# A transformer block with linear attention and top-2 experts: the router in natural layout, LayerNorm 2 through a PSUM bank, small steps moved between engines

## The reference, cut to what matters

```python
mod = (silu(c) @ wmod).reshape(2, 6, 1, -1)
sa, ca, ga, sb, cb, gb = mod[:, 0], ..., mod[:, 5]
ga, gb = (2 * (g >= 0) - 1) * maximum(abs(g), 0.25)        # for g in ga, gb
h = layernorm(x) * (1 + ca) + sa
Q, K, V = h @ Wq.T + bq, h @ Wk.T + bk, h @ Wv.T + bv      # 16 heads of 16
Q, K = elu(Q) + 1, elu(K) + 1
Z = 1 / (Q . sum_s(K) + 1e-6)                              # per token and head
x = x + ga * ((Q @ (K^T V) * Z) @ Wo.T + bo)
h = layernorm(x) * (1 + cb) + sb
logits = (h / |h|) @ (centroids / |centroids|).T + h @ w_route.T     # 8 experts
gates = softmax(logits where logits >= second largest, else -inf)
out_e = gelu(h @ w1[e] + b1[e]) @ w2[e] + b2[e]            # exact gelu
x = x + gb * sum_e gates[e] * out_e
```

## Time and profile before

| | us |
|---|---|
| three runs | 414.61, 415.77 (median), 416.47 |
| profiled execution | 416.12 |
| its span, first to last instruction | 414.3 |

### The profile page before, as it was taken

How to read it: one execution, slowest core, us unless ns; L and a number is a source line. 1 busy time by engine, 2 the same in 40 slices (tenths; PEclk the granted TensorE clock), 3 DMA queues, 4 the chain that set the end, 5 groups by cost and what they waited for, 6 DMA issues and landing times. The chain is left out here.

```text
span 414.3 us, 8993 instructions
## 1 busy us (share of the span) xinstructions
PE 359.5 (87%) x2610; PEld 329.2 (79%) x2610; DVE 340.4 (82%) x993; ACT 206.9 (50%) x451; POOL 254.0 (61%) x292
## 2 busy tenths in 40 slices
PE   4998899999996456889899899899898998998695
PEld 3477788888875446889889789789798898998695
DVE  4988778888779988898898898898998988986643
ACT  2256587787662144454554453454545544545341
POOL 2415778878766555766767758658667677465101
PEclk9999899999999977999999999999999999999999
DMA  8944000000000031132321421313223214223301
GB/s 264 331 147 127 2 0 0 0 0 2 1 2 0 1 102 53 52 108 54 97 79 52 127 73 54 117 61 76 93 66 96 77 52 126 78 56 124 105 26 52
DMA packets 23179, 30.36 MB, mean 73 GB/s; under 512 B 2258, under 2 KB 13938, under 8 KB 23156
## 3 DMA queue, kind: packets, MB, share of 16 engines
q1 hardware_dynamic: 22340, 29.03, 23.3%
q10 hardware_dynamic: 816, 1.05, 0.7%
HBM read 25.75 MB, written 4.33 MB: 73 GB/s over the span
## 5 line engine op out<-in xcount | busy, mean ns | idle before, releaser
L448 POOL TENSOR_TENSOR hid_pair<-hid_g,hid_pair 128x512 fp32r<-128x512 f32 x56 | 75.6, 1350 | 67.0 <-ACT hid_pair L619 67.0
L612 ACT ACTIVATE bank<-bank,cols_sb 128x256 f32<-128x256 f32 x128 | 51.3, 438 | 50.7 <-PE bank L662 50.5
L660 PE MATMUL bank<-tr_hi,w_hi 128*128 128x256 f32 x256 | 74.2, 290 | 0.0
L662 PE MATMUL bank<-tr_hi,w_lo 128*128 128x256 f32 x256 | 72.4, 283 | 0.0
L661 PE MATMUL bank<-tr_lo,w_hi 128*128 128x256 f32 x256 | 72.4, 283 | 0.0
L662 PE MATMUL bank<-w_hi,hid_pair 128*128 128x256 f32 x252 | 70.8, 281 | 0.0
L660 PE MATMUL bank<-w_hi,hid_pair 128*128 128x256 f32 x252 | 70.8, 281 | 0.0
L661 PE MATMUL bank<-w_lo,hid_pair 128*128 128x256 f32 x252 | 70.7, 280 | 0.0
L619 ACT ACTIVATE hid_pair<-hid_g 128x512 fp32r<-128x512 f32 x64 | 40.5, 632 | 31.4 <-DVE hid_g L1243 30.3
L1243 DVE TENSOR_TENSOR hid_g<-bank,g_bc 128x512 f32<-128x512 f32 x64 | 43.9, 686 | 10.3 <-ACT bank L612 8.7
L660 PEld LDWEIGHTS bank<-tr_hi,w_hi 128*128 128x128 f32 x256 | 49.1, 192 | 0.6
(11 more groups left out here) (153 smaller groups left out, 927.6 us busy)
## 6 DMA issues: line engine op xcount, KB each, us to landing
g_bc<-g_dram SPq DMA_DIRECT2D x64, 256.0 KB, 3.4
x_sb<-in_x SPq DMA_DIRECT2D x16, 256.0 KB, 3.0
out<-x_sb SPq DMA_DIRECT2D x15, 256.0 KB, 2.3
early<-in_wmod ACTq DMA_DIRECT2D x2, 512.0 KB, 8.0
q_sb<-in_w SPq DMA_DIRECT2D x2, 512.0 KB, 6.4
q_sb<-in_w SPq DMA_DIRECT2D x1, 1024.0 KB, 9.4
q_sb<-in_wqkvT SPq DMA_DIRECT2D x1, 768.0 KB, 6.7
early<-in_wmod SPq DMA_DIRECT2D x1, 512.0 KB, 3.9
```

Of the source, the lines that this page charges most:

```text
L448: gp.tensor_tensor(hid_lo[:, p, :, :], hid_g[:, p % 2, :, :], hid_hi[:, p, :, :].bitcast(F32), ALU.subtract).then_inc(e_hlo, 1)
L612: last = ac.activation(half, half, ACT.Gelu, bias=b1_sb[:, e:e + 1])
L660: te.matmul(out_ap, l_hi, r_hi, start=start, stop=False)
L662: return te.matmul(out_ap, l_lo, r_hi, start=False, stop=stop)
```

## The change

VectorE's share: `stats_of` ends with bn_aggr; `modulate_e` is two operations over both tiles, one in place in PSUM; `gates_a` has no transposes; `gates_b` writes one product; `denominators` loses the eps step and stands after gates_a; `scale_experts` is one operation. ScalarE gains `normalise_e` (x * rstd - mean * rstd into bank 7) and a second gate copy. POOL gains the negated mean, eps and neg_mr for LayerNorm 2, and `lo_gates`, and its order in the step changes. PE's router has the tokens stationary, and both tiles' expert sums share bank 6 (the last unit's second tile uses bank 7). b2's rows are its high, high and low parts at partitions 0, 32 and 64, to match the gates' high, low and high parts.

```diff
-        lgT = bank[1][0:4 * NE, 0:2 * P]
+        xn = bank[7][:, :].rearrange("p (t e) -> p t e", t=2)
+        lg = bank[1][:, 0:8 * NE].rearrange("p (t k) -> p t k", t=2)
+        def sums(u, t):
+            return bank[7][:, 0:E] if t == 1 and u.nth(NU - 1) else bank[6][:, t * E:(t + 1) * E]
+        def kv_bank(u):
+            return bank[2] if u.nth(NU - 1) else bank[6 + u.h]
@@ gpsimd
+            def make_rstd(u, eps, power, done):
+                h = u.h
+                gp.tensor_scalar(neg_mean[:, h, :], mv[:, h, :, 0], -1.0, None, ALU.mult)
+                gp.tensor_scalar(var_eps[:, h, :], mv[:, h, :, 1], LN_EPS, None, ALU.add).then_inc(eps, 1)
+                wait(pool, eps, u.count(1, 1))
+                gp.tensor_tensor(rstd[:, h, :], var_eps[:, h, :], minus_half[:, 0:2], ALU.pow).then_inc(power, 1)
+                wait(pool, power, u.count(1, 1))
+                gp.tensor_tensor(neg_mr[:, h, :], neg_mean[:, h, :], rstd[:, h, :], ALU.mult).then_inc(done, 1)
+            def lo_gates(u):
+                if not u.plus(-1) or u.nth(NU - 1):
+                    wait(pool, e_gexp, u.count(1, 1))
+                else:
+                    wait(pool, e_hlo, u.plus(-1).count(NP, 1))
+                if u.plus(3):
+                    wait(pool, o_qz, u.count(1, 4))
+                wait(pool, e_gThi, u.count(1, 1))
+                gp.tensor_tensor(gT_r[32:32 + NE, u.h, :], gT_f[0:NE, u.h, :], gT_r[0:NE, u.h, :].bitcast(F32),
+                                 ALU.subtract).then_inc(e_gTr, 1)
@@ gpsimd step_e, the order after the change
+                lo_e(u.plus(-1), 3); exp_gates(u.plus(1)); make_qz(u.plus(4)); lo_e(u, 0); lo_gates(u.plus(1))
+                lo_e(u, 1); norm_e(u.plus(2)); lo_e(u, 2); add_experts(u.plus(-1)); make_prod(u.plus(5))
+                rstd_e(u.plus(3))
@@ scalar
+            def normalise_e(u):
+                wait(act, e_rstd, u.count(1, 1))
+                if u.nth(0):
+                    act.wait_ge(a_acc, NU - 1)
+                wait(act, e_h, u.count(1, 0))
+                for t in range(2):
+                    last = ac.activation(xn[:, t, :], x_sb[:, u.tile(t), :], ACT.Identity,
+                                         bias=neg_mr[:, u.h, t:t + 1], scale=rstd[:, u.h, t:t + 1])
+                last.then_inc(e_xn, 1)
@@ keep_gates
-                ac.activation(gT_r[0:4 * NE, u.h, :], gT_f[:, u.h, :], ACT.Copy).then_inc(e_gTr, 1)
+                ac.activation(gT_r[0:NE, u.h, :], gT_f[0:NE, u.h, :], ACT.Copy).then_inc(e_gThi, 1)
+                ac.activation(gT_r[64:64 + NE, u.h, :], gT_f[0:NE, u.h, :], ACT.Copy).then_inc(e_gThi2, 1)
@@ scalar step_e: normalise_e(u+2) after gelu 1, before keep_gates(u+1)
@@ tensor, route
-                for c in range(NC):
-                    for k, part in enumerate((tr_hi, tr_lo)):
-                        last = te.matmul(lgT, route_r[:, c, :], part[:, h, c, :], ...)
+                for t in range(2):
+                    tok = slice(t * P, (t + 1) * P)
+                    for c in range(NC):
+                        te.matmul(lg[:, t, :], tr_hi[:, h, c, tok], route_r[:, c, :], start=(c == 0), stop=False)
+                        last = te.matmul(lg[:, t, 0:2 * NE], tr_lo[:, h, c, tok], route_r[:, c, 0:2 * NE],
+                                         start=False, stop=(c == NC - 1))
@@ vector, modulate_e
-                for t in range(2):
-                    ve.scalar_tensor_tensor(xc[:, t, :], x_sb[:, u.tile(t), :], mv[:, h, t, 0:1],
-                                            mod_row[:, b, 2, :], ALU.subtract, ALU.mult).then_inc(e_xc, 1)
-                for t in range(2):
-                    wait(dve, e_xc, u.count(2, t + 1))
-                    last = ve.scalar_tensor_tensor(nat[:, h, t, :], xc[:, t, :], rstd[:, h, t:t + 1],
-                                                   mod_row[:, b, 1, :], ALU.mult, ALU.add)
+                wait(dve, e_xn, u.count(1, 1))
+                shift_b, cb = (of_batch(mod_row[:, :, k, :], b).to_broadcast([P, 2, E]) for k in (1, 2))
+                TT(xn, xn, cb, ALU.mult).then_inc(e_xc, 1)
+                wait(dve, e_tp, u.count(1, -1))
+                wait(dve, e_sq, u.count(2, -2))
+                wait(dve, e_xc, u.count(1, 1))
+                TT(nat[:, h, :, :], xn, shift_b, ALU.add).then_inc(e_h, 1)
@@ gates_b
-                TT(g_nat[:, :, 3, :].bitcast(F32), g_sel, rec, ALU.mult)
-                TT(g_nat[:, :, 0:3:2, :], sel_twice, rec_twice, ALU.mult).then_inc(e_gnat, 1)
-                TT(g_nat[:, :, 1, :].bitcast(F32), g_nat[:, :, 3, :].bitcast(F32), g_nat[:, :, 0, :].bitcast(F32),
-                   ALU.subtract).then_inc(e_gnat, 1)
+                TT(g_nat[:, :, 0:NE], g_sel, rec, ALU.mult).then_inc(e_gnat, 1)
@@ make_prod and denominators: 17 columns per head, the last holds DEN_EPS
+                gp.tensor_tensor(prod[:, :, 0:D].rearrange("p (t h) d -> p t h d", t=2), q4, ks, ALU.mult)
-                ve.tensor_scalar(den_e[:, :, :], den[:, :, :], DEN_EPS, None, ALU.add).then_inc(o_den, 1)
@@ split_b2: four operations in place of six, on 8 partitions; one DMA for b2 in place of two
```

More of the change, by code:

```diff
@@ L506, in _ @@
             make_qz(unit(2))
+            make_prod(unit(3))
             add_bo(unit(NU - 4))
@@ L829, in route @@
                 wait(pe, e_lgn, u.count(1, 0))
-                for c in range(NC):
-                    for k, part in enumerate((tr_hi, tr_lo)):
-                        last = te.matmul(lgT, route_r[:, c, :], part[:, h, c, :],
-                                         start=(c == 0 and k == 0), stop=(c == NC - 1 and k == 1))
+                for t in range(2):
[4 more added lines that the diff above has]
+                                         start=False, stop=(c == NC - 1))
                 last.then_inc(e_route, 1)
@@ L877, in second_at_end @@
                         for w2_part in (w2_hi, w2_lo):
-                            te.matmul(bank[6 + t][:, 0:E], hid_hi[:, p, j, t * P:(t + 1) * P],
-                                      w2_part[:, 2 * p + j, :], start=False, stop=False)
+                            te.matmul(sums(unit(NU - 1), t), hid_hi[:, p, j, t * P:(t + 1) * P],
+                                      w2_part[:, 2 * p + j, :], start=False, stop=False, skip_group_check=True)
                 wait(pe, *lo_made(unit(NU - 1), p))
@@ L882, in second_at_end @@
                     for j in range(2):
-                        last = te.matmul(bank[6 + t][:, 0:E], hid_lo[:, p, j, t * P:(t + 1) * P],
-                                         w2_hi[:, 2 * p + j, :], start=False, stop=(j == 1))
+                        last = te.matmul(sums(unit(NU - 1), t), hid_lo[:, p, j, t * P:(t + 1) * P],
+                                         w2_hi[:, 2 * p + j, :], start=False, stop=(j == 1), skip_group_check=True)
                     last.then_inc(last_f2, 1)
@@ L942, in _ @@
             TT = ve.tensor_tensor
-            for rows in (bqk_r[:, :], b2_r[:, :], gT_r[:, :, :]):
+            for rows in (bqk_r[:, :], b2_r[:, :], gT_r[:, :, :], g_nat[:, :, :]):
                 last = ve.memset(rows.bitcast(F32), 0.0)
@@ L1251, in lo_hid @@
                     .then_inc(e_hlo_v, 1)
-            G = 6
+            G = 4
             def gates_a(u):
                 wait(dve, e_route, u.count(1, 1))
-                by_quarter = lgT.rearrange("k (t q j) -> k t q j", t=2, q=4)
-                for q in range(4):
-                    last = ve.transpose(lg[32 * q:32 * (q + 1), :, :], by_quarter[:, :, q, :])
-                last.then_inc(e_lgn, 1)
-                wait(dve, e_lgn, u.count(1, 1))
                 wait(dve, e_rn, u.count(1, 1))
```

178 lines of the change are left out of this document (84 added, 94 removed).

## The result

The changed kernel takes 390.94 us (median of four runs, 390.65 to 391.04), the kernel before 415.19 us in the same comparison; the ratio is 0.941, interval 0.938 to 0.944. The prediction said 391.

A forecast was written before the change was run, and what follows sets the result against it. VectorE was taken to bound the expert phase before, PE after; savings of 18.2 (twelve steps), 1.8, 0.2 and 4.7 us, together 24.9, took 416.12 to 391.2, stated as 391. The range was 386 to 402, PE-bound case 386 to 396.

The forecast's parts named there:

- The stalls of PE go, PE bounds: Steady expert steps: PE's waits before the b2 matmul and router vanish, step 14.64 us, twelve steps save 18.2 us.
- VectorE bounds the expert phase: Expert phase of the kernel before: VectorE, busy 14.40 of 16.27 us a step, is the bound, PE just behind.
- VectorE falls to 10.2 us: Steady expert step: VectorE loses 4.17 us of work, from 14.40 to 10.2 us.
- The modulation in PSUM at 0.686 each: VectorE, expert step: two 128x512 operations with one PSUM operand, 0.686 us each without GpSimd contention, saving 1.51 us.
- The router, +0.40: TensorE, expert step: eight router matmuls at 0.11 us, 0.88 in all, replace four taking 0.48, adding 0.40 us.
- The new wait for lo_gates costs nothing, half a us of slack: GpSimd's queue, expert step: lo_gates waits for transposed, copied gates; half a us of slack, so cost 0.
- Step 13, the transition, the tail: Savings in step 13 (1.8 us), up to unit 2's router (4.7) and in steps 14 and 15 (0.2).
- The attention phase at 0: Before 118 us: edits there gain 0, since PE is busy 6.03 of 6.03 us in steady units.
- GpSimd as the bound: Rival, expert steps: GpSimd's 12.7 us of work plus remaining idling make steps 15.4 us, 400 us total; chance 0.22.
- VectorE's wait for the normalised block: Rival, steady steps: ScalarE delivers the block late, VectorE waits, steps stay at 16.1 us, total 410; chance 0.11.
- The slower ring at 435: Rival, expert steps: the loop through GpSimd from exp_gates via lo_gates takes 18.3 us a step, total 435; chance 0.07.

The follow-up runs named there:

- b_router: The kernel before with only the new router in natural layout (tokens stationary, no VectorE transposes): 422.50 us, ratio 1.018.
- a_modulate_back: The changed kernel with LayerNorm 2's old modulation on VectorE and without ScalarE's normalise_e: 410.39 us, ratio 0.989.
- a_router_back: The changed kernel with only the old router: four matmuls of 256 columns and four VectorE transposes; 389.23 us, ratio 0.935.
- b_stats_pool: The kernel before with only the small statistics operations moved from VectorE to GpSimd (both for LayerNorm 1, eps alone for LayerNorm 2): 409.27 us, ratio 0.989.
- b_modulate: The kernel before with only the new modulation through PSUM, normalise_e, neg_mr on GpSimd and both tiles' sums in one bank: 396.67 us, ratio 0.955.
- a_pool_2x256: The changed kernel with two more GpSimd additions of 128x256 elements at the end of steps 0 to 14: 401.45 us, ratio 0.966.

## Why the prediction was right

**The stalls of PE go, PE bounds.** Shown by the windows after and by the two variants with less on PE. Predicted step 14.64, measured 14.66; twelve steps gave 17.9 us for 18.2. The bound is narrow: one ring through GpSimd and VectorE stands 0.3 us behind it.

**"VectorE bounds the expert phase."** Half right. The kernel before was bound by a ring, VectorE from gate 0 to `tr_lo`, then PE and ScalarE, not by VectorE's whole work. Its 1.04 us of transposes were not on it; counting them as part of what frees the step did no harm only because the sum was taken from PE's side. `b_router` is what tells the two apart.

**VectorE falls to 10.2 us.** It fell to 11.06. The operations were sized nearly right: over the twelve steps their durations add up to 16.0 us a step before and 12.0 after, 4.0 apart for 4.17. (The negated mean was priced at 0.567, a mean over both phases; in these steps it takes 0.39.) But neighbours overlap. In the rows above, operations of 0.69 us start 0.60 apart, and 1.44 and 1.90 us pairs last 3.19 together. I took a sum of durations (4.17) from a busy time that counts an overlap once (14.40); busy time fell by 3.34. It cost nothing here, since VectorE had over 3 us to spare.

**The modulation in PSUM at 0.686 each.** Measured 0.691 and 0.692, with GpSimd busy beside it. The old form depends on what GpSimd does. In `a_modulate_back` the pair of L1260 takes 1.44 us while GpSimd works; in the kernel before, the same pair took 0.87 while GpSimd stood idle from 290.89 to 292.30:

```profile
238.39 0.73 POOL L485 TENSOR_TENSOR gT_r<-gT_f,gT_r 8x256 fp32r<-8x256 f32 x1 [0.56 <-ACT gT_r L647]
239.42 1.53 POOL L460 TENSOR_TENSOR hid_pair<-hid_g,hid_pair 128x512 fp32r<-128x512 f32 x1 [0.30 <-ACT hid_pair L663]
```

```profile
289.60 1.29 POOL L409 TENSOR_TENSOR early<-q_sb,ksum_row 128x512 f32 x1
292.30 1.43 POOL L448 TENSOR_TENSOR hid_pair<-hid_g,hid_pair 128x512 fp32r<-128x512 f32 x1 [1.42 <-ACT hid_pair L619]
```

```profile
291.32 0.87 DVE L1222 SCALAR_TENSOR_TENSOR k_sb<-x_sb,mv,mod_row 128x256 f32 x2
292.11 1.91 DVE L1226 SCALAR_TENSOR_TENSOR nat<-k_sb,rstd,mod_row 128x256 f32<-128x256 f32 x2
```

Both engines' operations lengthen where they meet (1.53 and 1.43 for GpSimd's 1.29).

The rule of the Trainium skill (SBUF — State Buffer, Who interferes with whom), that an instruction with at most one SBUF input doesn't contend with GpSimd, agrees with these rows.

**The router, +0.40.** The eight take 0.81 us to the start of the next block, 0.11 apart, as the key-value matmuls of the earlier trace rows, and the second matmul of that block starts 0.20 after its first in place of 0.12. The whole is the 0.40 priced: a step of `a_router_back` in which PE has no wait is 14.26, one after the change 14.66. The 81 ns of the Trainium skill (TensorE: Matmul & The Clock Gate, Back-to-back issue gap) would have made it 0.65 us; the row decided rightly.

**The new wait for lo_gates costs nothing, half a us of slack.** Right, and close: from the additions on GpSimd the slack of the ring is about 0.3 us, and it is the branch over the squares that sets it, not the one over `lo_gates`. GpSimd is busy 12.45 us for 12.7, `lo_gates` takes 0.728 for 0.735, ScalarE 9.43 for 9.5. Measured from the start of first 0, `lo_gates` starts at 6.8 us (predicted 6.5), and `tr_lo` is done at 12.75 (13.1).

**Step 13, the transition, the tail.** 1.8, 4.7 and 0.2 predicted; 1.5, 4.1 (from the Q, K products of unit 15 to the router of unit 2, 51.18 us before and 47.11 after) and -0.3 measured. All three were somewhat too large. The transition also differs from one execution to the next: in the second profile of the same changed kernel it takes 1.4 us more, with PE at the lower clock for longer (mean granted clock 0.79 for 0.89). The profile before has 0.90 there, so the 4.1 compares like with like.

```profile
116.36:163.47 47.11, 32.74 (x215) 29.19 (x216) 35.01 (x95) 21.41 (x47) 33.87 (x47) 0.89 0.12 40
```

```profile
116.78:165.27 48.49, 35.62 (x215) 31.93 (x215) 35.28 (x95) 21.39 (x47) 33.91 (x47) 0.79 0.13 39
```

**The attention phase at 0.** Wrong by 2.2 us in the good direction (the products of unit 15 start at 118.54 before and 116.36 after), and this is what made the total come out. In the kernel before, the units that start at 34.69 and 42.86 took 8.17 and 7.59 us. In the first, PE was busy 6.29 us; in the second always, with 3.4 us of it at 1.2 GHz (granted clock 0.78 over the unit):

```profile
34.69:42.86 8.17, 6.29 (x39) 5.41 (x39) 7.50 (x26) 5.10 (x10) 3.79 (x6) 1.00 0.34 96
42.86:50.45 7.59, 7.59 (x38) 6.57 (x39) 4.91 (x14) 4.17 (x8) 5.40 (x7) 0.78 0.01 2
```

In the profile after no such stretch falls here, and the same units take 7.08 and 5.98. GpSimd's longer rstd did show once in the start-up, as the prediction allowed: from unit 0's products to unit 2's it is 16.72 us before, 17.45 after and 17.48 in `b_stats_pool`. The units behind it made up for that. In the second profile of the same changed kernel the stretch is back, on the unit before:

```profile
35.72:43.28 7.56, 7.56 (x38) 6.50 (x39) 5.88 (x17) 4.27 (x9) 4.95 (x8) 0.77 0.13 38
```

It is the move of LayerNorm 1's statistics that shortens this phase. From unit 0's products to unit 15's, the three profiles with the statistics whole on VectorE (the kernel before, `b_modulate`, `b_router`) take 100.5 to 100.6 us; `b_stats_pool`, which moves nothing else, takes 98.8; the ten profiles of the changed kernel and its variants take 98.1 to 98.6. The kernel before, then `b_stats_pool`:

```profile
17.97:118.54 100.57, 96.94 (x582) 83.55 (x581) 83.05 (x239) 70.77 (x133) 69.19 (x84) 0.98 0.13 38
```

```profile
16.88:115.65 98.77, 96.57 (x581) 83.53 (x580) 78.27 (x213) 70.51 (x133) 77.57 (x111) 0.98 0.14 41
```

PE was busy in the steady unit that the prediction looked at, but not in the first ones, where VectorE was the busier (7.50 of 8.17 us above) and PE waited. The slow stretch moves as well: it begins at 42.9 to 43.5 us in the first three profiles, at 35.3 in `b_stats_pool`, and in the ten others at 34.0 to 37.1 (seven) or nowhere before 136 (three). Earlier it falls where PE has idle time to lose: the two units together take 13.5 us there, 15.8 before. Why the clock falls at one place and not another stays open.

That the total is within 0.1 us is luck: errors of 0.3, 0.3, 0.6 and 0.5 us one way stand against 2.2 the other. The gain forecast was 24.9 us; the profiled pair shows 25.4, the medians 24.3.

**The rivals.** GpSimd as the bound (0.22) failed by 0.3 us a step, nearer than its price of 400 suggested; `a_pool_2x256`, with two additions more on GpSimd, shows what it looks like, at 401. VectorE's wait for the normalised block is 1.3 us in all. The slower ring at 435 was far off: of GpSimd's 5.0 us of idle time a step 2.2 are left (14.66 - 12.45).

## What to carry to other kernels

A busy share of nine tenths doesn't make an engine the bound: follow the ring once round, from an operation to the same one of the next step, and ask of each saving whether it stands in the ring. The same edit can be a loss alone (+0.41 us a step) and nearly free beside others, and the part that decides is the one that shortens the longest ring, here the modulation, with four fifths of the gain a step. Don't take summed durations from a busy time where neighbours overlap, and test a claimed slack by adding a known operation. When several things could have held an operation, take the one that ended just before it: the b2 product started 0.12 us after the scaled experts and 2.5 us after `lo_gates`.

## What the runs showed of the hardware

A stretch of 3.4 us at the lower of TensorE's two clock levels (1.2 GHz) was absent from the start-up in one profile of the changed kernel and began at 37.1 us in the other; it costs 1.6 us (7.59 for 5.98) where PE is busy anyway, and 0.5 (7.56 for 7.08) in the unit before, where PE has waits. A GpSimd operation on 8 partitions with 256 elements each (0.728 us) is no cheaper than one with 256 elements on 128 partitions (0.63 to 0.735). A TensorE pair of a 128-column weight load and 32 or 16 moving columns takes 0.11 us, no less than one with 128. VectorE's operations of 0.69 us start 0.60 us apart when nothing holds them.
